# Turning attention probabilities by VectorE blocks and DMA instead of TensorE, with a per-head minimum and a new order

## The reference

```python
# layer 0: 16 query heads over 1 key head, window +-64, then a gate, rmsnorm, centering
scores = q @ k.T / 4; scores = where(window, scores, -1e9); attn = softmax(scores) @ v
out = attn * gate + query * (1 - gate)
# layer 1: 3 neighbours per token, gathered by an index
w = square(relu(q . k_near / 4)); out = x + (w / sum(w)) @ v_near @ Wo.T
# layer 2: twice (sa on x itself, then ca on the context), 16 heads of 64
sim = (q @ k.T + rel_pos_bias) * 64 ** -0.5
attn = softmax(sim); x = x + attn @ v @ wo + bo
# layer 3: a gated state-space block (conv of 4 taps, decay, 8 heads), then 8-head attention
h = mamba(x); out = h + softmax(where(pad, -1e9, q @ k.T / sqrt(32))) @ v @ Wo
```

## Time and profile before

| | us |
|---|---|
| median of 3 runs | 1370.55 |
| lowest and highest run | 1367.40, 1371.41 |
| the profiled execution | 1367.05 |
| its span | 1365.0 |
| PE busy | 1269.3 (93%) |
| DVE busy | 962.6 (71%) |
| ACT busy | 788.3 (58%) |
| POOL busy | 338.6 (25%) |
| DMA moved | 44.42 MB, mean 33 GB/s |

### The profile page before, as it was taken

The page is one execution under the profiler, slowest core; times in us unless marked ns, Lnnn a source line. Parts: engine busy times, 40 slices in busy tenths (PEclk is TensorE's granted clock), DMA queues, the critical chain, the costliest instruction groups (busy, mean ns, idle before and its releaser), DMA issues.

```text
span 1365.0 us, 26220 instructions
## 1 busy us (share of the span) xinstructions
PE 1269.3 (93%) x9590; PEld 1006.6 (74%) x9590; DVE 962.6 (71%) x1877; ACT 788.3 (58%) x2690; POOL 338.6 (25%) x766
## 2 busy tenths in 40 slices
PE   6787899999999999999999999999999999988877
PEld 3466778788787778788777778788777777776655
DVE  3655768687787868687787868687787868482633
ACT  3153747475675757475665757475665757564331
POOL 2104131232314131222314131222314131212020
PEclk9899999999999999999999999999999999999898
DMA  8710101001010101001010101001010101000000
GB/s 266 283 43 1 43 1 40 12 8 42 0 46 4 46 4 38 12 8 42 0 46 4 46 4 38 12 8 42 0 46 4 46 4 35 5 5 5 5 4 4
DMA packets 28588, 44.42 MB, mean 33 GB/s; under 512 B 4710, under 2 KB 20614, under 8 KB 28044
## 3 DMA queue, kind: packets, MB, share of 16 engines
q1 hardware_dynamic: 26252, 31.41, 7.2%
q0 software_dynamic: 2304, 12.58, 2.6%
HBM read 37.65 MB, written 6.34 MB: 32 GB/s over the span
## 4 chain that ended last, share of the span: by engine, by line
PE 75%; DVE 14%; ACT 4%; POOL 3%; issue 2%; DMA 1%; SPq 0%; DVEq 0%; another core or an unknown queue 0%; POOLq 0%; ACTq 0%
PE psum L497 47%; PE psum L491 9%; PE psum L657 5%; PE psum L546 2%; PE psum L676 2%; PE psum L709 2%; DVE small_ L1025 2%; PE psum L721 2%; DVE A L1019 2%; DVE A L1033 1%; PE psum L753 1%; PE psum L566 1%; POOL small_ L1301 1%; ACT A L812 1%; DVE A L1110 1%
## 5 line engine op out<-in xcount | busy, mean ns | idle before, releaser
L1301 POOL TENSOR_SCALAR small_<-small_ 128x1 f32<-128x1 f32 x112 | 33.8, 302 | 732.1 <-DVE small_ L1037 354.7
L812 ACT ACTIVATE A<-A,small_ 128x128 f32<-128x128 f32 x384 | 148.6, 399 | 35.2 <-DVE small_ L1026 35.1
L805 ACT ACTIVATE A<-psum 128x1024 f32<-128x1024 f32 (+2 forms) x112 | 76.4, 682 | 119.7 <-PE psum L491 112.3
L491 PE MATMUL psum<-cst,A 128*128 128x128 f32 x672 | 107.0, 284 | 39.9 <-DVE A L1033 20.5
L491 PEld LDWEIGHTS psum<-cst,A 128*128 128x128 f32 x672 | 74.6, 142 | 68.3 <-DVE A L1033 24.7
L812 ACT ACTIVATE ca_p<-ca_p,small_ 128x128 f32<-128x128 f32 x256 | 98.7, 389 | 4.9 <-DVE small_ L1026 4.8
L812 ACT ACTIVATE sa_p<-sa_p,small_ 128x128 f32<-128x128 f32 x256 | 98.7, 388 | 0.8 <-DVE small_ L1026 0.6
L1190 DVE SCALAR_TENSOR_TENSOR A<-psum,half_cw,A 128x127 f32<-128x127 f32 (+2 forms) x288 | 75.2, 340 | 26.2 <-ACT A L916 26.2
L1019 DVE TENSOR_TENSOR A<-psum,cst 128x1024 f32<-128x1024 f32 x32 | 39.2, 1224 | 56.0 <-PE psum L546 54.2
L812 ACT ACTIVATION_READ_ACCUMULATOR A<-A,small_ 128x1 f32 x384 | 76.0, 198 | 0.0
L1302 POOL TENSOR_TENSOR small_<-small_,neg_half 128x1 f32<-128x1 f32 x112 | 67.7, 605 | 9.3
(11 more groups left out here) (219 smaller groups left out, 3214.3 us busy)
## 6 DMA issues: line engine op xcount, KB each, us to landing
inT<-in_tokT SPq DMA_DIRECT2D x16, 256.0 KB, 2.6
kv_rows<-A SPq DMA_DIRECT2D x16, 256.0 KB
ctx_in<-in_ctx SPq DMA_DIRECT2D x16, 128.0 KB, 2.1
A<-bias_rows SPq DMA_DIRECT2D x1, 2048.0 KB, 9.6
Wsakv<-in_wsa_kv SPq DMA_DIRECT2D x1, 2048.0 KB, 11.3
Wcakv<-in_wca_kv SPq DMA_DIRECT2D x1, 2048.0 KB, 9.4
ctx_end<-in_tokT SPq DMA_DIRECT2D x16, 128.0 KB, 2.2
out<-x_out SPq DMA_DIRECT2D x16, 128.0 KB, 1.7
```

What stands on the lines that cost most here:

```text
L491: mm = pe.transpose(out[:, c * P:(c + 1) * P], src[:, c * P:(c + 1) * P], ident)
L805: return act.activation(out, in_, ACT.Copy)
L812: ins = act.activation(p[:, h * T:(h + 1) * T], p[:, h * T:(h + 1) * T], ACT.Exp, bias=sm(part, "nm", w * HU + h, w * HU + h + 1), accum_o ...
L1301: then(pool.tensor_scalar(t, src, scale, eps, ALU.mult, ALU.add))
```

## The change

In four places:

1. **Turning in layer 2.** PE's transposes and ACT's copies of stage `p` go. After scaling, DVE transposes the 1024 columns in blocks of 32 x 32 (one instruction) into the tile of queries or keys. ACT issues a DMA that writes this tile (512 KB) to device memory. SP waits for it and issues 4 DMAs that read it back, with the four groups of 32 partitions exchanged, into the tile of probabilities. PE's stage `m` waits for these, and takes its operand in four runs of 32 columns per head. Layers 0 and 3 are turned by PE as before.
2. **The softmax's shift.** Scores are made negative (the scale on the queries, the bias and the masks change sign), and DVE does 8 instructions per unit, one per head of 128 columns, that add the bias and give the head's minimum as an accumulator. ACT computes exp(minimum - negated score). A count after each half (4 heads) lets ACT begin on the first half.
3. **Order.** New strings in `ORDER`; SP's loop is written by `SP_TURN`.
4. Two semaphores of POOL's rsqrt become one.

```diff
 ORDER = {
-    "PE": "3143412314323143241312412311241344314241412132421414",
...
+    "PE": "313413423143213243142142114244141434131112421414",
...
+SP_TURN = ["idx", "ca0", "ca1", "kv", "end", "tok", "sa0", "sa1", "ctx", "out"]
...
+            def move_probs(done, L, w):
+
+                sp.wait_ge(sem[f"{L}_blocks{w}"], done)
+                came = moving[L, w].ap().rearrange("(b k) (c n) -> c k b n", k=SQ, c=P // SQ)
+                to = (PA2, PB2)[w][L][:].rearrange("p (b n) -> p b n", b=P // SQ)
+                for c in range(P // SQ):
+                    sp.dma_start(to[c * SQ:(c + 1) * SQ], came[c]).then_inc(sem[f"{L}_moved{w}"], 16)
...
-                def turn_probs(w):
-                    def run(t):
-                        need_unit(t, f"{L}_probs", w)
-                        if w == 1:
-                            need_unit(t, f"{L}_PTsb", 0)
-                        turn(X, (PA2, PB2)[w][L], HU).then_inc(sem[f"{L}_PT"], 1)
-                    return run
-
                 def mix(t):
-                    need_unit(t, f"{L}_PTsb", 1)
                     for w in range(2):
+                        need_dma(t, f"{L}_moved", w)
...
+                                probs_T = in_blocks((PA2, PB2)[w][L])[:, :, slot, :]
...
                 part = PART[L]
-                need_unit(t, f"{L}_negmax", w)
                 for h in range(HU):
-                    ins = act.activation(p[:, h * T:(h + 1) * T], p[:, h * T:(h + 1) * T], ACT.Exp,
+                    if h % (HU // 2) == 0:
+                        need_lows(t, L, w, h // (HU // 2))
+                    ins = act.activation(p[:, h * T:(h + 1) * T], p[:, h * T:(h + 1) * T], ACT.Exp, scale=-1.0,
...
-                def turned(w):
+                def written(w):
                     def run(t):
-                        need_unit(t, f"{L}_PT", w)
-                        copy((Q2, K2)[w][L][:], X).then_inc(sem[f"{L}_PTsb"], 1)
+                        need_unit(t, f"{L}_probs", w)
+                        act.dma_start(moving[L, w].ap(), (Q2, K2)[w][L][:]).then_inc(sem[f"{L}_blocks{w}"], 16)
...
+            def softmax_low(t, L, w, p, scores, extra):
+
                 need_unit(t, f"{L}_scores", w)
-                ins = dve.tensor_tensor(heads(p), heads(scores), extra, ALU.add)
...
-                then(dve.tensor_reduce(mx, heads(p), AX.X, ALU.max))
-                dve.tensor_scalar(nm, mx, -1.0, None, ALU.mult).then_inc(sem[f"{L}_negmax"], 1)
+                held()
+                for h in range(HU):
+                    at = slice(h * T, (h + 1) * T)
+                    ins = dve.tensor_tensor_reduce(p[:, at], scores[:, at], extra(h), 1.0, TOP, ALU.add, ALU.min,
+                                                   sm(PART[L], "nm", w * HU + h, w * HU + h + 1))
+                    if h % (HU // 2) == HU // 2 - 1:
+                        ins.then_inc(sem[f"{L}_lows"], 1)
...
-                dve.tensor_tensor(heads(p), heads(p), each(rc, T), ALU.mult).then_inc(sem[f"{L}_probs"], 1)
+                ins = dve.tensor_tensor(heads(p), heads(p), each(rc, T), ALU.mult)
+                if L in LAYER:
+                    then(ins)
+                    need_unit(t, f"{L}_scores", 1)
+                    to = (Q2, K2)[w][L][:].rearrange("p (b h n) -> p h b n", h=HU, n=SQ)
+                    ins = dve.transpose(to, p.rearrange("p (h b n) -> p h b n", h=HU, n=SQ))
+                ins.then_inc(sem[f"{L}_probs"], 1)
```

More of the change, by code:

```diff
@@ L386, in need_unit, with need_lows, need_dma @@
                 eng.wait_ge(sem[name], t.n if name[:2] == "c3" else t.unit[w])
-            return need, free, need_unit
+            def need_lows(t, L, w, half):
+                eng.wait_ge(sem[f"{L}_lows"], t.value(2, half + 1) if L == "c3" else t.value(4, 2 * w + half + 1))
+            def need_dma(t, name, w):
+                eng.wait_ge(sem[f"{name}{w}"], t.value(64, 64))
+            return need, free, need_unit, need_lows, need_dma
         block = stack.enter_context(nc.Block())
@@ L435, in weights, with turn, at, during @@
                     sp.dma_start(dst[:], src.rearrange("(k p) n -> p k n", p=P)).then_inc(sem[name], 16)
+            def turn(i):
+                def at(n):
+                    return n if isinstance(n, int) else sp.snap(n)
+                def during(b):
+                    return not isinstance(b, int) or 0 <= b < B
+                def own(name):
+                    if name == "kv" and during(i + 3):
+                        store_kv(at(i + 4))
+                    elif name == "end" and during(i) and during(i + 1):
+                        load_ctx_end_next(i + 1, at(i + 2))
+                    elif name == "out" and during(i):
+                        store(i, at(i + 1))
+                    elif name in ("idx", "tok", "ctx") and during(i + 3) and during(i + 4):
+                        before, load = {"idx": ("near_at", load_idx), "tok": ("out0T", load_tokens), "ctx": ("cn_hat", load_ctx)}[name]
+                        sp.wait_ge(sem[before], at(i + 4))
+                        load(i + 4)
+                    elif name[:2] in LAYER and during(i + 2 - LAYER[name[:2]]):
+                        move_probs(at(16 * (i + 3 - LAYER[name[:2]])), name[:2], int(name[2]))
+                for name in SP_TURN:
+                    own(name)
             load_tokens(0)
@@ L462, in _ @@
             weights("wsa_in", zip(W2["sa"], (wsa_q, wsa_kv, wsa_o)))
-            load_next(1, 1)
+            turn(-3)
             weights("late_in", zip(W2["ca"], (wca_q, wca_kv, wca_o)))
@@ L467, in _ @@
             load_ctx_end(0)
-            for b in range(2, 4):
-                load_next(b, b)
+            for i in (-2, -1):
+                turn(i)
             with sp.Fori(0, B - 4) as i:
[L471 to L478, removed]
+                turn(i)
+            for i in range(B - 4, B):
+                turn(i)
             sp.wait_ge(sem["stored"], 16 * (B + 1))
@@ L485, in _ @@
             pe.sem_inc(sem["c3_kv"], 1)
[L486 removed]
+            need, free, need_unit, need_lows, need_dma = need_by(pe)
             def turn(out, src, n):
@@ L686, in layer2 @@
                 return {**own, f"{L}_hat": [turn_hat], f"{L}_q": [queries], f"{L}_k": [keys], f"{L}_v": [vals],
-                        **{f"{L}_s{w}": [scores(w)] for w in range(2)}, **{f"{L}_p{w}": [turn_probs(w)] for w in range(2)},
+                        **{f"{L}_s{w}": [scores(w)] for w in range(2)},
                         f"{L}_m": [mix], f"{L}_out": [project]}
@@ L894, in layer2 @@
                         **{f"{L}_s{w}": [lambda t, w=w: softmax(t, L, w, (PA2, PB2)[w][L])] for w in range(2)},
-                        **{f"{L}_p{w}": [turned(w)] for w in range(2)}, f"{L}_m": [moved(PA2, f"{L}_oT", f"{L}_oT_sb")]}
+                        **{f"{L}_p{w}": [written(w)] for w in range(2)}, f"{L}_m": [moved(PA2, f"{L}_oT", f"{L}_oT_sb")]}
             def m_squares(t):
@@ L962, in _ @@
             steps = [0]
-            need, free, need_unit = need_by(dve)
+            need, free, need_unit, need_lows, need_dma = need_by(dve)
             def step(ins):
@@ L1273, in _ @@
             steps = [0]
-            need_names, free, need_unit = need_by(pool)
+            need_names, free, need_unit, need_lows, need_dma = need_by(pool)
             def restart():
@@ L1468 @@
     kv_rows = nc.dram_tensor("kv_rows", (T + 2 * EDGE, 2 * D), F32)
-    build(nc, *args, bias_rows, kv_rows, out)
+    moving = {(L, w): nc.dram_tensor(f"moving_{L}{w}", (P, UNIT), F32) for L in ("sa", "ca") for w in range(2)}
+    build(nc, *args, bias_rows, kv_rows, moving, out)
     got = run_bass_kernel_spmd(nc, [arrays], core_ids=[0])
```

79 lines of the change are left out of this document (36 added, 43 removed).

## The result

The changed kernel takes 1442.62 us (median of 4 runs, 1440.6 to 1444.5), the kernel before 1368.97 beside it: ratio 1.0543, 95% interval 1.0506 to 1.0579. I had forecast 1362 us in a range of 1320 to 1398. It is slower, and outside the range.

What follows compares the result with a forecast made beforehand. PE bounds the kernel (74.72 of 76.54 us a turn); then the round ACT, DVE, memory, PE would. 14 x (76.1 - 76.54) = -6, ends -1, from 1367.05: 1360; median 3.5 above, so 1362 us, range 1320 to 1398.

Steps and rivals of the forecast that it cites:

- the walk: New turn followed from PE's first stage (ca_ctx) through ACT, DVE, memory and back to PE: 76.1 us.
- Steps 1 and 2: PE to the end of ca_hat, 13.5 us; then ACT's scalings, 8 exponentials and first tap, reaching 20.95 us.
- Step 3: DVE's gapless chain from first tap to c3's minimum, 41.6 us with hand-overs; sa's second transpose ends at 60.4.
- my lower end: DVE's minimum: lowest cost considered for one head's add-and-read pair, 0.21 us, or 1.7 us per unit.
- ScalarE's exponential with its read: Likeness used to price DVE's pair at its first instruction's 0.28 to 0.29 us, 2.3 us per unit.
- the 0.59 us step: DVE's 512-column add from PSUM gives way after 0.59 us; from it, a head's step is at least 0.21.
- Rival B: DVE's pair costs 0.37 us or more (3.0 per unit); turn 78.9, kernel slower at 1402 us; chance 0.22.
- Step 4: sa's trip through memory, 7.4 us, ending at 67.8; PE waits about 0.5 us for the second unit's probabilities.
- Rival C: Trip through memory takes 9 us, a read back delayed in SP's queue; turn 77.7, 1386 us; chance 0.12.
- Step 5: PE from the second half of sa_m to the turn's end: 7.1 plus 1.0 us, reaching 75.9.
- The ends: Outside full turns: earlier exponentials save 1.3 us in two or three softmaxes, trips cost 2 to 3; together -1.
- 5 us of PE standing still a turn: PE's waits in the new order, some 5 us a turn, first at hat3/gate0, then at sa_m.

Runs made afterwards that it cites:

- run 6: Changed kernel with SP's transfers reordered: kv store ahead of the reads of ca's second unit, token load behind both reads of sa; 1376.0 us, 1.0074.
- run 9: Changed kernel with only SP's token load moved behind both reads of sa, kv store still behind ca's reads; 1423.9 us, 1.0415.
- Run 5: Changed kernel with 9 idle products on PE between the halves of sa_m, to fill its wait; 1412.0 us, 1.034.
- run 7: Kernel before's orders with the new minimum, ca alone through memory, sa turned by PE, ca_m behind center0; 1374.1 us, 1.0062.
- run 2: Changed kernel with sa and ca both turned by PE, nothing through memory, new minimum and new order kept; 1429.2 us, 1.0434.
- run 8: Changed kernel with the kernel before's engine orders, ca_m behind center0, sa and ca both through memory, SP's queue as changed; 1466.3 us, 1.0743.
- run 10: run 6 with back0, center0 and c3_p earlier on PE, and c3_p earlier on ACT; 1421.2 us, 1.0392.
- run 11: Changed kernel with ca through memory, sa turned by PE, earlier order behind ca_m, kv store ahead of ca's second unit; 1406.7 us, 1.029.
- run 12: run 8 with SP's queue of run 6; 1419.7 us, 1.0391.
- run 1: Changed kernel with sa turned by PE again, ca still through memory, new minimum and order kept; 1402.85 us, 1.0257.

## Why the prediction was wrong

I measure from PE's first stage, 683.96 in the turn above, as the walk did.

- **Steps 1 and 2 held.** First tap at 705.56, 21.6 us in; the walk had 21.05.
- **Step 3 gave the right end for a wrong reason.** `sa`'s last transpose ends at 744.18, 60.2 us in; I had 60.4. But the pair costs 0.21 us, my lower end, so a unit takes 1.7 us and not 2.3: 2.4 us less in the four units up to there. DVE works 36.2 us where I had 38.3, but stands still for 2.4 where I had 1.0 for the hand-overs; 1.4 of the 2.4 are one wait for PE's scores of `ca`. These errors cancelled nearly, which is luck. ScalarE's exponential with its read the earlier trace rows was the wrong likeness; the bound from the 0.59 us step was the right one. Rival B's dear pair is refuted; that the kernel is slower came true for other reasons. The transpose, 1.25 us against 1.2, held.
- **Step 4 failed: the trip is 10.6 us, not 7.4.** The write leg took 6.4 in place of 3.8, the read leg 4.25 in place of 3.6. I had put both together from transfers that mostly run alone. `sa_q`'s write, with little beside it, takes 2.6 us, less than my 3.8; `sa_k`'s finds the gather and the first unit's reads in front of it, and these reads had the token load (issued at 741.36) in front of them. Run 6 takes the gather and the token load away and gets 8.3 us; the read leg stays at 4.3 there, so 0.7 of the 3.2 us is no collision but a leg sized too small. PE came to `sa_m` 65.6 us in (I had 66.4) and waited 4.2 us, not 0.5. Rival C had the trip at 9 us, still too short, and from SP's queue. My argument against it, that each of SP's waits is over in time, was true and beside the point: the read was not late in SP's queue, the write began late on the DMA engines. The Trainium skill ("DMA: Bandwidth & Descriptors", "Issuing engines are not separate DMA queues") says that transfers started by scalar, sync or gpsimd "will ultimately run on the same 16 DMA engines and interleave with each other". The trace agrees on the sharing, and runs 6 and 9 with 4.0 and 5.5 us for this write in the turns shown. It interleaves less than that sentence suggests: none of `sa_k`'s 144 packets moved while the gather's did. One sum of the prediction is wrong as well: with a trip of 6.4 us in place of 7.4 the walk's turn would be 0.45 us shorter, not 1, since PE itself comes to the second half only at 67.35.
- **Step 5 failed: 10.9 us from the second half of `sa_m` to the end, not 8.1.** I named the clock among the things that would make me wrong and gave it no term. Run 5 shows it to be 2.8 us. The trip's 3.2 and the clock's 2.8, less 0.2 in the chain and the 0.2 of small waits that I had added at the end, make 5.6 of the 5.7 us between 76.1 and 81.8: this turn is accounted for.
- **The ends.** I had -1 us for all that is not a full turn. The first store alone comes 18.7 us late, one of the full turns included, and PE's mean clock up to 260 us is 0.90 against 0.96 before. In run 6, with SP's other list, it comes 6.5 us late; more was not taken apart.
- **The order.** "5 us of PE standing still a turn" was too low (7.3, of which 3.1 are waits for DVE); that `ca`'s trip is covered was right: PE waits for it 0.2 us in the whole program. The price, seen in run 7, is the place of `ca_m`. What I did not see is that the new order's own waits, 0.67 at `m_hat`, 1.01 at `hat3`, 0.52 at `turn1` and 0.52 at `near_q`, are there without any trip (run 2).
- **The minimum** I priced at a gain of half a unit in "two or three softmaxes". Alone it takes PE's waits from 1.8 to 0.6 us a turn and 35 us off the kernel. The Trainium skill ("VectorE: DVE Perf Modes", on the TRN2 errata) advises tiles of 512 elements or more; here 8 ops of 128 columns from PSUM with the reads, 1.7 us, beat the two of 1024 and the negation, 2.59. The measurement decides for this edit. It does not speak against large tiles as such: one pass over the scores in eight pieces was set against two passes, and one pass in one piece was not run.

Open: the gather was never moved alone, its 47 us are the difference of runs 6 and 9, and part of them is the clock, which falls in every turn of run 9 and in one of the twelve of run 6. A read straight from SBUF to SBUF, without the second leg, was not tried.

## What to carry to other kernels

A transfer on the critical path has to be priced with everything that flies beside it; look which unit of it is waited for, and let the collision fall on the other. Ask of each new wait of PE how long it is: one of 4.2 us cost 2.8 us more in slow products. And when work is taken from the bound engine, look whether that engine holds the turn at that place: run 7 took 1.8 us from PE where DVE's chain held it, got them back as waits, and paid for the later place of `ca_m`.

## What the runs showed of the hardware

- In the main loops the granted clock fell in every turn with a PE wait of 3.1 us or more (the changed kernel, runs 8, 9 and 10) and of 2.43 to 2.55 in runs 11 and 12. With 2.52 (run 7) it fell in eight turns of twelve, with 1.92 in eleven of thirteen in run 2 and in four of thirteen in run 1. In run 6 it stayed at 1.00 behind 1.51, 1.87 and 2.29 us, but fell in one turn whose waits were 0.33 to 0.68 us, several in a row (turn 78.8 in place of some 76.8). So no length of a single wait separates the two cases here, and a wait of about 2 us may cost twice in one turn and once in another.
- A DVE op with an accumulator of 128 columns lasts 0.29 us and steps by 0.21; its read (0.08) lies beside the next op.
- The same 512 KB write took 2.6 to 6.3 us by what was in flight. Its first packet came 0.8 us behind the issue in one case and 3.2 in the other.
